# Product keys in a two-layer decoder: row one-hots kept two groups at a time, every key row in split form

## The chip, the core and the metric

The program runs on one core of a Trainium2 chip. The metric is the time of one execution on the device in microseconds (us). The engines are PE (matrix products; its weight loads are listed apart as PEld), DVE (vector), ACT (scalar activations and copies), POOL (GpSimd) and SP (which issues the transfers). They run in parallel, each its own instructions in order, and wait for one another through semaphores.

## What is computed

A decoder of two layers over x of 16 x 128 tokens, 256 wide: causal attention, attention to a context, a product-key layer, gated attention, aligned attention, and a mixture of 16 experts. The change touches the product-key layer alone. Cut to what matters, with 8 heads, nk = 64, k = 8:

```python
xn = batch_norm(inputs) * gamma + beta
q = (xn @ w_q.T).reshape(b, n, 2, h, kd).transpose(2, 0, 1, 3, 4)
sim = jnp.einsum('pbnhd,hkpd->pbnhk', q, keys)
s, i = jax.lax.top_k(sim, k)
...  # sums of the two halves' best, the best 8 of the 64 sums
scores, pk = jax.lax.top_k(all_scores, k)
idx = jnp.take_along_axis(all_idx, pk, axis=-1)
o = jnp.einsum('bnd,bnhkd->bnhk', inputs, key_in[idx])
o = gelu(o) * softmax(scores)
return jnp.einsum('bnhk,bnhkd->bnd', o, key_out[idx])
```

## The kernel before

Tokens are taken in 16 tiles of 128, two tiles (t = 0 and t = 1) to a pair, 8 pairs. The kernel doesn't gather: it computes the gelu of the products with all 4096 rows of key_in and multiplies them by a matrix of weights that is zero where a key isn't chosen. The stage (stage_product_keys, line 1982) has a preparation and then a loop over pairs, whose last turn is written out.

**Preparation.** key_in is turned by PE in 16 jobs (turn_in) of four 128 x 128 blocks. ACT rounds a job to fp32r (kiT high) and DVE subtracts (kiT low); of the rows 24 to 31 (SPLIT = 24) only a plain fp32 copy is kept, in kiT_rest: those four jobs (WHOLE) come ahead of the loop. The loop over pairs (line 2049, in_jobs) has two jobs in turns 0 to 3 and one in turns 4 to 7, and beside it normalises the tokens (ACT, fp_xn), turns them (PE) and collects statistics (DVE).

**A pair on PE.** Sixteen activation steps (activations, line 2361), each 2 rows of keys x 2 halves of the width, fill a bank that ACT empties with a gelu (L2447). A split row takes three fp32r products (split_product, line 583: high·high, high·low, low·high); in four steps, rows 24 to 31, it is one plain fp32 product (L2371). After step 0 the codes of the first tile are turned (turn_codes, L2354); after steps 3 to 6 come the similarities of the pair's second tile (SIMS_AT = 3). Then come four weight groups of the first tile (weight_group, L2391): a group is 16 of the 64 token columns of both halves, 64 small f16 products of row one-hots (row_hot, the stationary side) with column one-hots (col_hot). The next pair's similarities stand between them. Then the outputs of the first tile (L2404, f_out), with the second tile's four groups put between its 32 products at 23, 24, 26 and 28 (SECOND_AT), and last the outputs of the second tile (f_turn).

**A pair on DVE.** one_hot (line 2534) makes column one-hots (L2565 to L2570) and then all row one-hots of a tile in one instruction (L2573). choose (line 2458) finds the best keys from the similarities; weigh (line 2520) divides the exponentials that ACT made and releases the turning of codes. apply_weights (line 2576) multiplies each group's weights into gel, in two instructions (L2586); PE's groups 2 and 3 wait for the application of groups 0 and 1, whose banks they reuse, and the outputs for all four. The order is one_hot(0), choose(1), apply 0 of tile 0, weigh(1), apply 1 to 3, one_hot(1), apply of tile 1, residual, choose and weigh of the next pair.

**POOL** makes the low parts of the next pair's two inputs, xb_pair (L2284) and hT_pair (L2290), each as soon as ACT has rounded the high part.

## Time and profile before

| what | us |
|---|---|
| median of 3 runs | 2009.88 (2009.46 to 2011.67) |
| the profiled execution, own time | 2011.48 |
| its span | 2009.8 |
| PE busy in it | 1842.6 (92%) |
| DVE busy | 1327.1 (66%) |
| ACT busy | 649.5 (32%) |
| POOL busy | 175.8 (9%) |
| mean granted clock of PE | 0.964 |

The span runs from the first to the last instruction. A busy share is a mean over six stages with different limits. The product-key layer takes the time from 538 (preparation) over 582 (first pair) to 1141. In rows in order of time the first number is the start from the beginning of the span, the second the length in us; xN is the number of instructions merged in a row, and brackets give the idle time of the engine before it and what ended it. Granted clock 1.00 is 2.4 GHz, 0.5 is 1.2 GHz.

### The profile page before, as it was taken

The numbers are of one execution on the slowest core, as the hardware profiler recorded it, in microseconds if no ns is written. First come the engines' busy times: TensorE is split into PE (matmuls) and PEld (weight loads), VectorE is DVE, ScalarE is ACT, GpSimd is POOL, SyncE is SP. The second block draws the span as 40 slices with busy tenths as digits, with TensorE's granted clock in tenths as the row PEclk, the third lists the DMA queues.
The fourth block names the chain that finished last, engine by engine and source line by source line (L and its number), as shares of the span: only waits on it lengthen the run. The fifth ranks groups of instructions, "written<-read, shape, count | busy, mean of one in ns | idle before, by whom it ended". The sixth has DMA issues, their size and how long they took to land. (4 is left out here: it accounts for less than half of the span.)

```text
span 2009.8 us, 43767 instructions
## 1 busy us (share of the span) xinstructions
PE 1842.6 (92%) x16819; PEld 1541.4 (77%) x16819; DVE 1327.1 (66%) x3598; ACT 649.5 (32%) x1504; POOL 175.8 (9%) x125
## 2 busy tenths in 40 slices
PE   6999999699749999999999878878899999999998
PEld 5887787477638888888888645557788888888887
DVE  4555555377668988888988446646666666666664
ACT  3444434244342211221122035426333333323332
POOL 0000000011000000000000046531000000000000
PEclk9999999799879999999999879979899999999999
DMA  4000000222060000000000130001212010111101
GB/s 159 1 1 0 0 0 1 48 64 63 1 131 8 8 7 3 7 7 8 3 7 1 35 85 1 0 1 38 33 16 32 16 31 16 29 18 27 20 0 43
DMA packets 139319, 48.61 MB, mean 24 GB/s; under 512 B 108178, under 2 KB 138418, under 8 KB 139186
## 3 DMA queue, kind: packets, MB, share of 16 engines
q1 hardware_dynamic: 139186, 46.66, 10.4%
q8 instruction: 105, 1.72, 0.4%
q14 instruction: 28, 0.23, 0.0%
HBM read 42.43 MB, written 4.19 MB: 23 GB/s over the span
## 5 line engine op out<-in xcount | busy, mean ns | idle before, releaser
L2849 DVE TENSOR_TENSOR m_act_up<-m_silu,m_up 128x512 f32<-128x512 f32 x136 | 93.5, 687 | 168.0 <-PE m_up L587 125.0
L2768 ACT ACTIVATE m_silu<-m_gate 128x512 f32<-128x512 f32 x136 | 81.5, 599 | 379.6 <-PE m_gate L587 379.6
L2833 DVE SCALAR_TENSOR_TENSOR g_x<-m_y,m_combine,g_x 128x256 f32<-128x256 f32 x272 | 118.8, 479 | 52.8 <-PE m_y L587 51.3
L233 ACT ACTIVATE a_prob<-a_score,a_neg_max 128x128 f32<-128x128 f32 x256 | 90.7, 367 | 170.3 <-DVE a_neg_max L223 170.3
L2404 PE MATMUL f_out<-f_ko,f_gel 128*128 128x256 f32 x512 | 123.9, 394 | 2.4 <-issue 1.3
L2447 ACT ACTIVATE f_gel<-f_act 128x512 f32<-128x512 f32 x128 | 76.6, 598 | 131.7 <-PE f_act L587 90.9
L2404 PE MATMUL f_turn<-f_ko,f_gel 128*128 128x256 f32 x512 | 111.8, 379 | 0.0
L2404 PEld LDWEIGHTS f_out<-f_ko,f_gel 128*128 128x128 f32 x512 | 96.1, 194 | 17.1 <-issue 4.1
L587 PE MATMUL f_act<-f_hT_pair_high,f_kiT_high 128*128 128x256 f32 x384 | 108.2, 282 | 0.0
L2404 PEld LDWEIGHTS f_turn<-f_ko,f_gel 128*128 128x128 f32 x512 | 97.3, 190 | 13.2
L587 PE MATMUL f_act<-f_hT_pair_high,f_kiT_low 128*128 128x256 f32 x384 | 107.3, 279 | 0.0
L587 PE MATMUL f_act<-f_hT_pair_low,f_kiT_high 128*128 128x256 f32 x384 | 107.3, 279 | 0.0
L2839 DVE TENSOR_TENSOR m_hidden_low<-m_act_up,m_hidden_high 128x512 fp32r<-128x512 f32 x136 | 93.2, 685 | 1.5
L1281 POOL TENSOR_TENSOR a_inv<-a_ss,a_inv_power 128x64 f32<-128x64 f32 x8 | 84.6, 10571 | 71.7 <-DVE a_ss L1485 71.7
L2762 ACT CAST m_hidden_high<-m_act_up 128x512 fp32r<-128x512 f32 x136 | 83.4, 613 | 18.9 <-DVE m_act_up L2849 18.9
L587 PE MATMUL m_y<-g_wT_high,m_hidden_high 128*128 128x256 f32 x288 | 81.9, 284 | 2.9 <-DVE g_x L2833 1.9
L587 PE MATMUL m_y<-g_wT_high,m_hidden_low 128*128 128x256 f32 x288 | 81.8, 284 | 0.0
L587 PE MATMUL m_y<-g_wT_low,m_hidden_high 128*128 128x256 f32 x288 | 81.5, 283 | 0.0
L587 PE MATMUL a_ring<-a_xnT_high,a_w_high 128*128 128x256 f32 x256 | 77.1, 301 | 4.5 <-DVE a_w_low L544 4.4
L2437 ACT ACTIVATE g_shared<-g_shared 128x64 f32<-128x64 f32 x16 | 4.1, 256 | 235.8 <-DVE g_shared L2483 235.7
L587 PE MATMUL m_y<-m_wT_high,m_hidden_high 128*128 128x256 f32 x256 | 73.0, 285 | 1.9 <-DVE g_x L2833 1.9
L587 PEld LDWEIGHTS f_act<-f_hT_pair_high,f_kiT_high 128*128 128x128 f32 x384 | 72.0, 188 | 2.8 <-ACT f_gel L2447 1.4
(381 smaller groups left out, 5010.0 us busy)
## 6 DMA issues: line engine op xcount, KB each, us to landing
f_gel<-in_L_ffn_key_in SPq DMA_DIRECT2D x16, 256.0 KB, 4.9
f_ko<-in_L_ffn_key_out SPq DMA_DIRECT2D x2, 2048.0 KB, 18.5
g_shared<-in_ctx SPq DMA_DIRECT2D x8, 256.0 KB, 2.8
fp_wq_nat<-in_L_ffn_w_q SPq DMA_DIRECT2D x8, 256.0 KB, 3.1
h_kept<-fp_hT SPq DMA_DIRECT2D x8, 256.0 KB, 2.9
g_shared<-h_kept SPq DMA_DIRECT2D x8, 256.0 KB, 3.4
g_ctx_next<-in_ctx SPq DMA_DIRECT2D x8, 256.0 KB, 2.7
g_ctx_all<-in_ctx SPq DMA_DIRECT2D x1, 2048.0 KB, 10.3
```

What stands on the lines that cost most here:

```text
L233: last = act.activation(self.prob[:, u % 4, j, :], self.score_bank[u % 2][:, j // 2, (j % 2) * P:(j % 2 + 1) * P], ACT.Exp, bias=self.neg_ ...
L587: ins = pe.matmul(dst, left[a], right[b], start=first and n == 0, stop=last and n == 2)
L1281: pool.tensor_tensor(inv[par][:, :], ss[par][:, :], inv_power[:, :], ALU.pow).then_inc(inverse_ready, 1)
L2404: last = pe.matmul(out_of(t), gel[:, r, t * P:(t + 1) * P], ko[:, r, :], start=(r == 0), stop=(r == R - 1))
L2437: act.activation(weight[:, :, :], weight[:, :, :], ACT.Exp).then_inc(weight_exp, 1)
L2447: act.activation(gel[:, rows_of(u):rows_of(u) + 2, :].rearrange("p r t -> p (r t)"), act_bank[q][:, :], ACT.Gelu).then_inc(act_used[q].sem, 1)
L2762: act.copy(hidden[0][:, g % 2, m, :], act_up[:, m, :]).then_inc(high_ready[m].sem, 1)
L2768: act.activation(silu[:, m, :], gate_bank[m][:, :], ACT.Silu).then_inc(silu_ready[m].sem, 1)
L2833: last = dve.scalar_tensor_tensor(x[:, tile, :], y_bank[n][:, t * D:(t + 1) * D], weight, x[:, tile, :], ALU.mult, ALU.add)
L2839: dve.tensor_tensor(hidden[1][:, g % 2, m, :], act_up[:, m, :], hidden[0][:, g % 2, m, :], ALU.subtract).then_inc(low_ready[m].sem, 1)
L2849: dve.tensor_tensor(act_up[:, m, :], silu[:, m, :], up_bank[m][:, :], ALU.mult) \
```

## The change

All 32 rows of keys are kept in split form, kiT_rest is gone, and all sixteen activation steps are split products, in the order of the rows. The 16 turning jobs of the preparation all go through the loop, two in each turn. To make room, row_hot keeps two groups instead of four (8 KB less in each partition): DVE makes groups 0 and 1 in one instruction at the end of one_hot, and group m + 2 after it has applied group m, ahead of the weighing. PE waits for row one-hots (row_ready) at groups 2 and 3 too. POOL's low part of hT_pair also waits for the first row one-hots of the second tile of the pair before. The second tile's similarities come after steps 2 to 5.

```diff
-        self.kiT = [s.sb(f"kiT_{part}", [P, KD, self.SPLIT, P], F32R) for part in ("high", "low")]
-        self.kiT_rest = s.sb("kiT_rest", [P, KD, self.R - self.SPLIT, P])
+        self.kiT = [s.sb(f"kiT_{part}", [P, KD, self.R, P], F32R) for part in ("high", "low")]
...
-                if n < WHOLE:
-                    return n // 2, SPLIT + 4 * (n % 2)
-                return (n - WHOLE) // 6, 4 * ((n - WHOLE) % 6)
+                return n // 8, 4 * (n % 8)
...
-                return range(WHOLE + 2 * i, WHOLE + 2 * i + 2) if i < 4 else range(WHOLE + i + 4, WHOLE + i + 5)
+                return range(2 * i, 2 * i + 2)
...
-                for n in range(WHOLE):
-                    turn_in(n)
...
-                for n in range(WHOLE):
-                    k, r = in_rows(n)
-                    act.wait_ge(in_turned[n % 2], n // 2 + 1)
-                    act.copy(kiT_rest[:, k, r - SPLIT:r - SPLIT + 4, :].rearrange("p r c -> p (r c)"), in_bank[n % 2][:, :]) \
-                        .then_inc(in_done[n % 2], 1)
...
-        row_hot = s.sb("row_hot", [P, HALF, P], F16)
+        row_hot = s.sb("row_hot", [P, 2, GT, P], F16)
...
-        hot_ready = s.sem("hot_ready")
+        row_ready = s.counting("row_ready", GU - 1)
...
-        TURN_AT, SIMS_AT, SECOND_AT = 0, 3, (23, 24, 26, 28)
+        TURN_AT, SIMS_AT, SECOND_AT = 0, 2, (23, 24, 26, 28)
...
                     pool.wait_ge(h_high, i + 1)
+                    if not (isinstance(i, int) and i == 0):
+                        pool.wait_ge(row_ready.sem, row_ready.at(2 * i - 1, 1))
                     pool.tensor_tensor(hT_pair[1][:, :, :], h_pair[:, :, :], hT_pair[0][:, :, :],
                                        ALU.subtract).then_inc(h_low, 1)
...
-            return 2 * ((step + SPLIT // 2) % (R // 2))
+            return 2 * step
...
-                            if r < SPLIT:
-                                last = split_product(pe, dst, [part[:, k, r, :] for part in kiT],
-                                                     [part[:, k, :] for part in hT_pair], k == 0, k == KD - 1)
-                            else:
-                                last = pe.matmul(dst, kiT_rest[:, k, r - SPLIT, :], h_pair[:, k, :],
-                                                 start=(k == 0), stop=(k == KD - 1))
+                            last = split_product(pe, dst, [part[:, k, r, :] for part in kiT],
+                                                 [part[:, k, :] for part in hT_pair], k == 0, k == KD - 1)
...
-                    pe.wait_ge(hot_ready, n + 1)
+                    pe.wait_ge(row_ready.sem, row_ready.at(n, 1))
...
+                    if m >= 2:
+                        pe.wait_ge(row_ready.sem, row_ready.at(n, m))
...
-                                last = pe.matmul(weight_bank(m, q)[:, j * R:(j + 1) * R], row_hot[rows, GT * m + j, :],
+                                last = pe.matmul(weight_bank(m, q)[:, j * R:(j + 1) * R], row_hot[rows, m % 2, j, :],
...
+            def row_hots(at, groups):
+
+                slot = at % 2
+                dve.tensor_tensor(by_twos(row_hot[:, slot:slot + groups, :, :].rearrange("p m t c -> p (m t) c")),
+                                  per_token(code_twice[:, 0, GT * at:GT * (at + groups), :], P),
+                                  numbers(P, GT * groups), ALU.is_equal).then_inc(row_ready.sem, 1)
+
+            def next_row_hots(i, t, m):
+
+                n = 2 * i + t
+                for q in range(2):
+                    dve.wait_ge(g_ready[q].sem, g_ready[q].at(n, m + 1))
+                row_hots(m + 2, 1)
...
-                dve.tensor_tensor(by_twos(row_hot[:, :, :]), per_token(code_twice[:, 0, :, :], P), numbers(P),
-                                  ALU.is_equal).then_inc(hot_ready, 1)
+                row_hots(0, 2)
...
+                    if m + 2 < GU:
+                        next_row_hots(i, t, m)
                     after(m)
```

On DVE, in the loop over pairs, first tile, from the application of group 0 (f_g) to that of group 3 (f_act); f_weight_sum and g_shared are the weighing. Before:

```order
L2586 SCALAR_TENSOR_TENSOR f_gel<-f_g,f_gel 128x32x16 x2
L2526 TENSOR_REDUCE f_weight_sum<-g_shared 128x8
...
L2527 RECIPROCAL f_weight_sum<-f_weight_sum 128x8
...
L2529 SCALAR_TENSOR_TENSOR g_shared<-g_shared,f_weight_sum 128x64 x2
...
L2586 SCALAR_TENSOR_TENSOR f_gel<-f_act,f_gel 128x32x16 x2
...
L2586 SCALAR_TENSOR_TENSOR f_gel<-f_g,f_gel 128x32x16 x2
...
L2586 SCALAR_TENSOR_TENSOR f_gel<-f_act,f_gel 128x32x16 x2
```

and after the change:

```order
L2587 SCALAR_TENSOR_TENSOR f_gel<-f_g,f_gel 128x32x16 x2
L2535 TENSOR_TENSOR f_row_hot<-f_code_twice,f_iota_half 128x2048
L2514 TENSOR_REDUCE f_weight_sum<-g_shared 128x8
...
L2515 RECIPROCAL f_weight_sum<-f_weight_sum 128x8
...
L2517 SCALAR_TENSOR_TENSOR g_shared<-g_shared,f_weight_sum 128x64 x2
...
L2587 SCALAR_TENSOR_TENSOR f_gel<-f_act,f_gel 128x32x16 x2
L2535 TENSOR_TENSOR f_row_hot<-f_code_twice,f_iota_half 128x2048
...
L2587 SCALAR_TENSOR_TENSOR f_gel<-f_g,f_gel 128x32x16 x2
...
L2587 SCALAR_TENSOR_TENSOR f_gel<-f_act,f_gel 128x32x16 x2
```

Two row one-hot instructions of 128x2048 have moved in, one ahead of the weighing and one ahead of the application of group 2.

On PE, in the loop over pairs, the first matmul of the first tile's groups 0 to 3 (f_g and f_act in turn), the turning of codes and the first output, with what each waits for. Before:

```order
L2391 MATMUL f_g<-f_col_hot,f_row_hot 128x32 [waits f_col_ready,f_hot_ready]
...
L2391 MATMUL f_act<-f_col_hot,f_row_hot 128x32 [waits f_act_used1,f_act_used0]
...
L2391 MATMUL f_g<-f_col_hot,f_row_hot 128x32 [waits f_g_used1,f_g_used0]
...
L2391 MATMUL f_act<-f_col_hot,f_row_hot 128x32 [waits f_g_used1,f_g_used0]
...
L2354 MATMUL f_turn<-g_ident,g_shared 128x128 [waits f_codes_copied,f_codes_ready]
L2354 MATMUL f_turn<-g_ident,g_shared 128x128 x2
...
L2404 MATMUL f_out<-f_ko,f_gel 128x256 [waits f_out_used0,f_g_used1,f_g_used0]
```

and after the change:

```order
L2379 MATMUL f_g<-f_col_hot,f_row_hot 128x32 [waits f_col_ready,f_row_ready]
...
L2379 MATMUL f_act<-f_col_hot,f_row_hot 128x32 [waits f_act_used1,f_act_used0]
...
L2379 MATMUL f_g<-f_col_hot,f_row_hot 128x32 [waits f_row_ready]
...
L2379 MATMUL f_act<-f_col_hot,f_row_hot 128x32 [waits f_row_ready]
...
L2344 MATMUL f_turn<-g_ident,g_shared 128x128 [waits f_codes_copied,f_codes_ready]
L2344 MATMUL f_turn<-g_ident,g_shared 128x128 x2
...
L2392 MATMUL f_out<-f_ko,f_gel 128x256 [waits f_out_used0,f_g_used1,f_g_used0]
```

The groups stand where they stood; groups 2 and 3 now name row one-hots as what they wait for.

## Rows read from the trace of the kernel before

**Rows 1.** Windows: busy us (instructions) of PE, PEld, DVE, ACT, POOL; granted clock, DMA, GB/s.

```profile
665.50:732.90 67.40, 67.06 (x847) 58.94 (x847) 59.36 (x231) 14.68 (x24) 2.59 (x2) 1.00 0.02 6
...
1098.20:1105.20 7.00, 4.44 (x260) 3.88 (x259) 6.83 (x20) 2.14 (x3) 0.00 (x0) 0.94 0.02 5
1105.28:1118.30 13.02, 13.02 (x46) 10.74 (x46) 9.48 (x10) 0.00 (x0) 0.00 (x0) 0.77 0.00 1
```

**Rows 2.** Tile f_kiT_rest: count, duration ns min/median/max, first and last start.

```profile
L2371 PE MATMUL f_act<-g_shared,f_kiT_rest x256: 378/379/635, 582.3 to 1078.2; 128*128 128x256 f32 x128
```

**Rows 3.** ACT in order of time, the gelus; columns: start us, length us, instruction.

```profile
671.22 0.60 ACT L2447 ACTIVATE f_gel<-f_act 128x512 f32<-128x512 f32 x1 [1.13 <-PE f_act L2371]
672.94 0.60 ACT L2447 ACTIVATE f_gel<-f_act 128x512 f32<-128x512 f32 x1 [1.13 <-PE f_act L2371]
...
682.81 0.60 ACT L2447 ACTIVATE f_gel<-f_act 128x512 f32<-128x512 f32 x1 [0.81 <-PE f_act L587]
684.22 0.60 ACT L2447 ACTIVATE f_gel<-f_act 128x512 f32<-128x512 f32 x1 [0.81 <-PE f_act L587]
```

**Rows 4.** PE in order of time, first tile's weights and start of outputs.

```profile
692.85 0.96 PE L2391 MATMUL f_g<-f_col_hot,f_row_hot 64*128 64x32 f16 x64
...
696.43 0.97 PE L2391 MATMUL f_g<-f_col_hot,f_row_hot 64*128 64x32 f16 x64
...
698.44 1.01 PE L2391 MATMUL f_act<-f_col_hot,f_row_hot 64*128 64x32 f16 x64
...
700.86 10.17 PE L2404 MATMUL f_out<-f_ko,f_gel 128*128 128x256 f32 x46 [0.20 <-issue]
```

**Rows 5.** DVE in order of time, the same stretch.

```profile
693.85 1.29 DVE L2586 SCALAR_TENSOR_TENSOR f_gel<-f_g,f_gel 128x512 f32<-128x512 f32 x2 [0.19 <-PE f_g L2391]
...
695.65 1.44 DVE L2529 SCALAR_TENSOR_TENSOR g_shared<-g_shared,f_weight_sum 128x64 f32<-128x64 f32 x2
697.02 1.28 DVE L2586 SCALAR_TENSOR_TENSOR f_gel<-f_act,f_gel 128x512 f32<-128x512 f32 x2
698.22 1.27 DVE L2586 SCALAR_TENSOR_TENSOR f_gel<-f_g,f_gel 128x512 f32<-128x512 f32 x2
```

**Rows 6.** DVE, start of a choosing, last column one-hots, row one-hots.

```profile
680.00 0.06 DVE L2464 MEMSET f_spare<- 1x1 f32 x1 [2.15 <-PE f_sim L587]
...
705.25 1.23 DVE L2570 TENSOR_TENSOR f_col_hot<-f_col_hot,f_w_twice 128x2048 f16<-128x2048 f16 x1
706.39 4.42 DVE L2573 TENSOR_TENSOR f_row_hot<-f_code_twice,f_iota_half 128x8192 f16<-128x8192 f16 x1
```

**Rows 7.** POOL in order of time, the two subtractions.

```profile
687.94 1.29 POOL L2284 TENSOR_TENSOR f_xb_pair_low<-g_shared,f_xb_pair_high 128x512 fp32r<-128x512 f32 x1 [58.32 <-ACT f_xb_pair_high L2318]
695.71 1.30 POOL L2290 TENSOR_TENSOR f_hT_pair_low<-g_shared,f_hT_pair_high 128x512 fp32r<-128x512 f32 x1 [6.48 <-ACT f_hT_pair_high L2323]
```

**Rows 8.** PE, second tile's groups 0, 2 and 3 between output matmuls.

```profile
710.96 0.96 PE L2391 MATMUL f_g<-f_col_hot,f_row_hot 64*128 64x32 f16 x64
...
714.44 0.97 PE L2391 MATMUL f_g<-f_col_hot,f_row_hot 64*128 64x32 f16 x64
...
716.40 0.96 PE L2391 MATMUL f_act<-f_col_hot,f_row_hot 64*128 64x32 f16 x64
```

**Rows 9.** ACT in the preparation, first instruction of three turns.

```profile
558.10 1.12 ACT L2149 ACTIVATE fp_xn<-g_x,fp_token_shift,fp_token_rstd 128x256 f32<-128x256 f32 x2
...
560.52 1.14 ACT L2149 ACTIVATE fp_xn<-g_x,fp_token_shift,fp_token_rstd 128x256 f32<-128x256 f32 x2
...
562.45 1.15 ACT L2149 ACTIVATE fp_xn<-g_x,fp_token_shift,fp_token_rstd 128x256 f32<-128x256 f32 x2
```

**Rows 10.** DVE in the last pair, last instructions of the weighing.

```profile
1101.04 0.36 DVE L2529 SCALAR_TENSOR_TENSOR g_shared<-g_shared,f_weight_sum 128x64 f32<-128x64 f32 x2
```

**Rows 11.** PE in the last pair, group 0 and the outputs.

```profile
1098.24 0.96 PE L2391 MATMUL f_g<-f_col_hot,f_row_hot 64*128 64x32 f16 x64
...
1105.28 13.11 PE L2404 MATMUL f_out<-f_ko,f_gel 128*128 128x256 f32 x46 [1.09 <-DVE f_gel L2586]
```

## Prediction of the time after the change

> **What bounds the kernel now.** I read the page's busy shares first, then the stretch of stage windows, then one pair of tiles in order of time on PE and DVE. Over a middle pair, 67.4 us long, PE is busy 67.06 us at full granted clock, while DVE is busy 59.36 us [rows 1]. So PE sets the time of a pair, DVE has 8 us to spare in all, and what counts is where DVE's work stands. The eight pairs repeat one another closely, so one pair is worked out and multiplied. T below is the start of the first weight matmul of a pair's first tile (692.85 in the pair shown [rows 4]); W is the same of its second tile (710.96 [rows 8]).
>
> **The key rows.** Before, four of the sixteen activation steps of a pair are plain fp32: two records of PE for each matmul, 256 in all for 8 pairs of four steps with four matmuls each [rows 2]. ACT's gelus follow the steps, so their distance is PE's time for a step: 672.94 − 671.22 = 1.72 us for a plain one, 684.22 − 682.81 = 1.41 us for a split one [rows 3]. The change turns the four into split ones: 4 × (1.72 − 1.41) = 1.25 us off PE in each pair, 10.0 us in eight. Both ends are measured on the very engine, so I allow only 9.5 to 10.5. (In the first pair one of the four hides behind a wait for codes, but the clock is half there and the others save more.)
>
> The Trainium skill (FP8 and Floating Point Precision, section TensorE Precision Notes) says that true fp32 takes four passes through the array. A split product takes three. By that a split step would cost three quarters of 1.72, or 1.29 us, and four of them in eight pairs would save 13.8 us, not 10.0. The trace doesn't agree: the ratio is 0.82.
>
> **The preparation.** The four key blocks that were only copied (before the loop, while ACT waited for the token statistics anyway) now go through the loop as rounded ones, so turns four to seven of the loop do two jobs, not one. The loop runs at ACT's pace. Its turn with two jobs takes 560.52 − 558.10 = 2.42 us, with one 562.45 − 560.52 = 1.93 us [rows 9]. Four turns at 0.49 are +2.0 us, all on the path, since the stage's pairs begin only when it is over. Bounds: 1.5 (DVE's end unchanged) and 2.6 (one more remainder of DVE at the tail).
>
> **The row one-hots, first tile.** This is the part that decides. DVE made all four groups in one instruction of 4.42 us [rows 6], long before T. Now two groups are made early, and group 2 and group 3 each only after group 0 and group 1 have been applied, between the applications. The trace has no row one-hot of one group. The same kind of instruction on 128x2048 f16, the column one-hots, takes 1.23 us, and the next one starts 706.39 − 705.25 = 1.14 us after it [rows 6]; a quarter of 4.42 would be 1.11, with the start-up of each instruction left out. I take 1.22 busy and 1.14 between starts.
>
> DVE's order after the change: apply group 0, one-hots 2, the three instructions that weigh the second tile, apply 1, one-hots 3, apply 2, apply 3. Start to start, an application of two instructions costs 698.22 − 697.02 = 1.20 [rows 5]. The weighing costs 2.1 us before, because its last two instructions take 1.44 us [rows 5] while POOL's low part runs, 695.71 to 697.01 [rows 7]. In the last pair, where POOL has no low part to make, the same two take 0.36 us [rows 10]. The change makes POOL's low part wait for the second tile's one-hots, in the middle of the output matmuls, where DVE has nothing to do until W + 1. So the weighing costs 0.76.
>
> The Trainium skill (SBUF — State Buffer, section Who interferes with whom) says that a DVE instruction with both inputs in SBUF and a GpSimd one that reads SBUF lock each other out. The trace agrees: 0.36 against 1.44 us.
>
> The sum: application 0 starts at T + 1.00 as before [rows 4, 5]; one-hots 2 run from 2.21 to 3.43; PE may start group 2 at 3.54 and reaches it at 3.58 anyway, as before [rows 4], so nothing is lost there. Weighing from 3.35, application 1 at 4.11 (before 4.17), one-hots 3 from 5.32 to 6.54. PE starts group 3 at T + 6.64; before, 698.44 − 692.85 = 5.59 [rows 4]. Application 3 needs that group's last matmul, at 7.64: it runs 7.67 to 8.96, and the outputs, which wait for it, start at T + 9.04; before, 700.86 − 692.85 = 8.01 [rows 4]. **PE loses 1.03 us** in each of seven pairs, 7.2 us. In the last pair no similarities of a next pair fill PE's gaps and no POOL was in the way, so it started its outputs at 1105.28 − 1098.24 = 7.04 [rows 11]; the new chain of DVE gives the same 9.04, so that pair loses 2.0. Together +9.2 us. Bounds: with one-hots at 1.11 and no latency, 0.8 a pair; with 0.1 us for each added wait of DVE and PE, 1.3: 7.0 to 11.5.
>
> **The second tile.** From W: application 0 at 1.00, one-hots 2 ready at 3.43, PE on group 2 at 3.54 (before 714.44 − 710.96 = 3.48 [rows 8]); application 1 at 3.35, one-hots 3 from 4.56 to 5.78, PE on group 3 at 5.88 (before 716.40 − 710.96 = 5.44 [rows 8]). Everything behind it moves by 0.44 us: 8 × 0.44 = +3.5 us; bounds 0.3 and 0.6 each, 2.4 to 4.8. One-hots of two groups (2.3 us, between 1.23 and 4.42) end by T + 16.9 and PE asks for them at T + 19.1, so the later start of that chain costs nothing.
>
> **The second similarities.** Moved from step three to step two, with the saving, they end at some 2.7 us earlier on PE. DVE waited 2.15 us for them before choosing [rows 6], and from there to application 0 (693.85 [rows 5]) it went on without a wait but the last 0.2 us. The choosing takes some 13.7 us and now ends 1.6 us before application 0 (2.7 earlier on a T that is 1.25 earlier, and the 0.2). It costs PE nothing and buys slack alone. POOL's other subtraction (687.94, 1.29 us [rows 7]) now meets DVE's matching instructions, which read two tiles of SBUF; that can hold DVE by 0.7 us, and the slack covers it.
>
> **The sum:** −10.0 + 2.0 + 9.2 + 3.5 = **+4.7 us**. The profiled execution has a span of 2009.8 us and its own time 2011.48; the median of the runs is 2009.88, so I add to the median: **2014.6 us**. The bounds added in the same direction reach from about 2010.5 to 2019. A change within 0.2% (4.0 us) is about what a measurement of this kernel can't tell from none.
>
> **The rivals.**
> The granted clock falls. In the last pair PE is busy only 4.44 of 7.00 us around the weights, and then the clock falls: 46 records of outputs take 13.0 us at a mean of 0.77 instead of 10.1 in a middle pair [rows 1, 4, 11]: from 2.4 to 1.2 GHz for part of it. One fall costs 2.9 us. The change puts a gap of 1.4 us before group 3 and one of 0.35 before the outputs into every pair. Against: similarities and weights stand between the gaps, and PE stays busy some 7.3 of 9 us. If half of the pairs fall, +10 us: 2025; one fall is inside my own range. Chance 0.12.
> DVE is held by POOL while it chooses, and the slack isn't there: 0.7 × 7 = +5 us, 2019.5. It decides from 1.6 us of delay on. Chance 0.08.
> POOL's low part still meets the weighing (the change doesn't do what it says): 1.08 × 7 = +7.6, 2022. The order of POOL speaks against it. Chance 0.04.
> Split steps run by their number of passes, as three quarters of the plain ones: −13.8 in place of −10.0, 2010.8. The gelus' distances speak against it. Chance 0.04.
> DVE isn't late (the other side): PE never waits for one-hots 3. That takes their end by T + 5.4, where I have 6.54; if DVE's gaps hid 1.1 us there and 0.4 at the second tile, the two waits would vanish: 2009.9 − 10.0 + 2.0 + 1 = 2003. For it speaks only that DVE is less busy than PE; against it that from application 0 to the outputs DVE's rows show not one wait [rows 5]. Chance 0.08.
>
> **How the numbers follow.** The forecast has 0.61; about two thirds of it lie over 2013.9, one third between 2009 and 2013.9, by the bounds of the two waits. The rest, 0.03, is left for what I haven't thought of, near no change. Slower by over 0.2%: 0.40 + 0.12 + 0.08 + 0.04 = 0.64. Within 0.2%: 0.21 + 0.04 + 0.03 + a little of the last rival, 0.29. Faster: 0.07. The range leaves out the last rival and the clock's upper half: 2009.5 to 2023.
>
> **What would show it.** Right: gelus 1.41 apart in all sixteen steps; the weighing's two instructions at 0.36 us in every pair; PE idle about 1.4 us before group 3 of the first tile and 0.4 before that of the second, put down to DVE's row one-hots; outputs 9.0 us after T; the preparation 2.0 us longer; a pair of 67.6 us. Wrong: group 3 starting under T + 5.7; granted clock under 1.00 in the middle pairs; DVE choosing until application 0.

## The result, and the profile after the change

The changed kernel takes **2015.85 us** (median of 11 runs, 2012.65 to 2023.99); the kernel before, in as many runs beside it, 2009.46 (2007.41 to 2011.67). The ratio is 1.0036, 95% interval 1.0025 to 1.0046: slower by 0.36%, outside the 0.2% that count as no change. Run once more beside the experiments it took 2017.62 (ratio 1.0044, 1.0027 to 1.0061). The forecast was 2014.6, in 2009.5 to 2023, slower. Time and sign came out; two terms of the sum did not, and they are what the experiments are about.

The profiled execution of the changed kernel (span 2019.6) is one of its longer ones; that of the second measurement (span 2014.4) is called the second trace. First the windows of the changed kernel: from one second tile's first weight matmul to the next pair's, then the two pieces of the last pair, to be held against [rows 1]. Columns as there: busy us (instructions) of PE, PEld, DVE, ACT, POOL; granted clock, DMA, GB/s.

```profile
717.84:785.67 67.83, 66.16 (x863) 58.51 (x864) 59.09 (x234) 14.65 (x24) 2.55 (x2) 1.00 0.02 6
1106.73:1116.09 9.36, 4.79 (x261) 4.20 (x260) 8.19 (x16) 2.14 (x3) 0.00 (x0) 0.73 0.01 2
1116.09:1128.70 12.61, 12.61 (x46) 10.44 (x46) 7.35 (x10) 0.00 (x0) 0.00 (x0) 0.80 0.01 1
```

A pair grew from 67.4 to 67.8 us while PE's work in it fell from 67.06 to 66.16: PE now waits 1.7 us of it. Where, is seen on PE in order of time, first tile (answers to [rows 4]; start us, length us, instruction, idle time before it and what ended it):

```profile
698.73 0.96 PE L2379 MATMUL f_g<-f_col_hot,f_row_hot 64*128 64x32 f16 x64
...
702.32 0.97 PE L2379 MATMUL f_g<-f_col_hot,f_row_hot 64*128 64x32 f16 x64
...
705.30 0.96 PE L2379 MATMUL f_act<-f_col_hot,f_row_hot 64*128 64x32 f16 x64 [1.12 <-DVE f_row_hot L2535]
...
707.74 0.45 PE L2392 MATMUL f_out<-f_ko,f_gel 128*128 128x256 f32 x1 [0.25 <-issue]
```

With T = 698.73, group 2 starts at T + 3.59 (forecast 3.58), group 3 at T + 6.57 (6.64), the outputs at T + 9.01 (9.04; before 8.01). The 1.12 us ahead of group 3 are put down to the row one-hots. DVE in the same stretch (answers to [rows 5, 6]):

```profile
699.73 1.29 DVE L2587 SCALAR_TENSOR_TENSOR f_gel<-f_g,f_gel 128x512 f32<-128x512 f32 x2 [0.63 <-PE f_g L2379]
700.94 1.22 DVE L2535 TENSOR_TENSOR f_row_hot<-f_code_twice,f_iota_half 128x2048 f16<-128x2048 f16 x1
...
702.55 0.36 DVE L2517 SCALAR_TENSOR_TENSOR g_shared<-g_shared,f_weight_sum 128x64 f32<-128x64 f32 x2
702.83 1.28 DVE L2587 SCALAR_TENSOR_TENSOR f_gel<-f_act,f_gel 128x512 f32<-128x512 f32 x2
704.03 1.21 DVE L2535 TENSOR_TENSOR f_row_hot<-f_code_twice,f_iota_half 128x2048 f16<-128x2048 f16 x1
705.16 1.28 DVE L2587 SCALAR_TENSOR_TENSOR f_gel<-f_g,f_gel 128x512 f32<-128x512 f32 x2
...
713.23 2.28 DVE L2535 TENSOR_TENSOR f_row_hot<-f_code_twice,f_iota_half 128x4096 f16<-128x4096 f16 x1
```

The chain has no gap: one-hots of one group 1.22 us (1.13 start to start), of two 2.28, the weighing's last two instructions 0.36 instead of 1.44. POOL stands out of their way now (answer to [rows 7]), and the second tile loses 0.30 us ahead of its last group (answer to [rows 8]; W = 717.84, group 3 at W + 5.81, before 5.44):

```profile
715.59 1.27 POOL L2280 TENSOR_TENSOR f_hT_pair_low<-g_shared,f_hT_pair_high 128x512 fp32r<-128x512 f32 x1 [20.49 <-DVE f_row_hot L2535]
```

```profile
723.65 0.96 PE L2379 MATMUL f_act<-f_col_hot,f_row_hot 64*128 64x32 f16 x64 [0.30 <-DVE f_row_hot L2535]
```

**Where the time stands.** The product-key layer cut at starts that every trace has: first turning of keys, first similarity, W of the eight pairs, last output product (us):

| piece | before | changed | changed, second trace |
|---|---|---|---|
| preparation, to the first similarity | 38.16 | 43.90 | 40.68 |
| from there to W of the first pair | 66.38 | 66.10 | 65.99 |
| six periods from W to W | 405.34 | 407.96 | 409.08 |
| seventh period (into the last pair) | 69.45 | 70.72 | 70.16 |
| last W to the last output product | 21.77 | 22.32 | 22.32 |
| sum | 601.10 | 611.00 | 608.23 |

The layer begins at 538.98, 540.01 and 538.01 us, and the stages behind it take 869.7, 868.6 and 868.1 us, so they give 1.1 to 1.6 back. The preparation, forecast with +2.0, costs 2.5 in one trace and 5.7 in the other; it is the first open question. The second is the pairs. A period without a fall of the clock is 67.83; before, the six have a mean of 67.56, the shortest 67.40. The added waits of 1.00 and 0.37 us fit the forecast, so the key rows gave only 0.9 to 1.1 of the forecast 1.25 (1.37 less 0.43, held against the shortest period, or less 0.27, held against the mean).

### The profile page after: what moved, and what is told of

Same layout as the page of the kernel before. It is cut to its first block and busy times, and to the rows that moved or that the text cites. A ratio compares the mean times of both kernels' runs of the same rounds, so it can differ in the third digit from the quotient of the medians.

```text
span 2019.6 us, 44141 instructions
## 1 busy us (share of the span) xinstructions
PE 1841.8 (91%) x16947; PEld 1547.6 (77%) x16947; DVE 1327.6 (66%) x3634; ACT 648.6 (32%) x1504; POOL 176.3 (9%) x125
## 3 DMA queue, kind: packets, MB, share of 16 engines
q8 instruction: 105, 1.72, 0.3%
## 5 line engine op out<-in xcount | busy, mean ns | idle before, releaser
L587 PE MATMUL f_act<-f_hT_pair_high,f_kiT_high 128*128 128x256 f32 x512 | 147.0, 287 | 0.2
L587 PE MATMUL f_act<-f_hT_pair_low,f_kiT_high 128*128 128x256 f32 x512 | 144.0, 281 | 0.0
L587 PE MATMUL f_act<-f_hT_pair_high,f_kiT_low 128*128 128x256 f32 x512 | 144.0, 281 | 0.0
L587 PEld LDWEIGHTS f_act<-f_hT_pair_high,f_kiT_high 128*128 128x128 f32 x512 | 97.2, 190 | 4.7 <-ACT f_gel L2435 1.6
L587 PEld LDWEIGHTS f_act<-f_hT_pair_low,f_kiT_high 128*128 128x128 f32 x512 | 97.1, 190 | 1.6
L587 PEld LDWEIGHTS f_act<-f_hT_pair_high,f_kiT_low 128*128 128x128 f32 x512 | 97.4, 190 | 0.0
```

What stands on the lines that cost most here:

```text
L587: ins = pe.matmul(dst, left[a], right[b], start=first and n == 0, stop=last and n == 2)
```

## Experiments

Each runs beside the kernel before on the same chip; every diff is against the changed kernel, unless it says otherwise. The periods are from W to W; "layer" is the sum of the table above (changed 611.0 and 608.2, before 601.1).

### The changed kernel again

> The changed kernel once more, as the reference for the others on the same chip. Its first trace has the preparation (from its first turning of keys to the first similarity) at 43.91 us, before 38.16: 5.75 longer, where the prediction had 2.0. If that excess belongs to the kernel, this execution shows 43 to 44 again, with the granted clock at half through the first 20 us of the preparation; if it was chance of one execution, 40 to 41. In the pairs: third group 3.6 and fourth 6.6 us behind the first tile's first weight matmul, outputs at 9.0, a pair of 67.8 us. Total 2014 to 2018.

Measured: 2017.62 us; preparation 40.68. So the excess has more than one size in one and the same kernel. The turnings of key_in and the fused products (of the keys with w_q, 128x64 each on PE) tell them apart. Before:

```profile
540.84 3.76 PE L2086 MATMUL fp_in_bank<-g_ident,f_gel 128*128 128x128 f32 x16
544.39 3.80 PE L2093 MATMUL fp_key_bank<-fp_keysT,fp_wq_nat 128*128 128x64 f32 x32
```

Changed, first trace, PE, then ACT behind it:

```profile
542.62 7.09 PE L2088 MATMUL fp_key_bank<-fp_keysT,fp_wq_nat 128*128 128x64 f32 x32 [0.68 <-ACT fp_keysT L2128]
549.50 1.91 PE L2081 MATMUL fp_in_bank<-g_ident,f_gel 128*128 128x128 f32 x8
551.21 3.52 PE L2088 MATMUL fp_key_bank<-fp_keysT,fp_wq_nat 128*128 128x64 f32 x16
```

```profile
554.76 0.59 ACT L2124 CAST f_fused_high<-fp_key_bank 128x512 fp32r<-128x512 f32 x1 [2.48 <-PE fp_key_bank L2088]
...
559.45 0.59 ACT L2124 CAST f_fused_high<-fp_key_bank 128x512 fp32r<-128x512 f32 x1 [1.55 <-PE fp_key_bank L2088]
```

Second trace:

```profile
540.62 7.09 PE L2088 MATMUL fp_key_bank<-fp_keysT,fp_wq_nat 128*128 128x64 f32 x32 [0.68 <-ACT fp_keysT L2128]
547.50 1.88 PE L2081 MATMUL fp_in_bank<-g_ident,f_gel 128*128 128x128 f32 x8
549.21 1.91 PE L2088 MATMUL fp_key_bank<-fp_keysT,fp_wq_nat 128*128 128x64 f32 x16
```

The same 16 products take 1.91 or 3.52 us. The first 18 us of the preparation as windows (columns as above; the granted clock is the third number from the end), before, changed and second trace:

```profile
538.98:556.98 18.00, 16.61 (x129) 15.65 (x130) 12.65 (x45) 11.53 (x22) 2.98 (x2) 0.84 0.01 2
```

```profile
540.01:558.01 18.00, 17.32 (x89) 17.14 (x90) 10.78 (x42) 7.03 (x13) 2.99 (x2) 0.50 0.01 1
```

```profile
538.01:556.01 18.00, 16.79 (x112) 16.37 (x112) 12.49 (x45) 8.64 (x17) 2.98 (x2) 0.69 0.01 1
```

Before, the clock was at 1.2 GHz until 5.7 us into the preparation and at 2.4 for the rest of these 18 us; now it stays at 1.2 for 11.2 or for 18.0 us. A rise at 11.2 costs some 0.4 us: ACT starts its first turn 10.22 us into the preparation instead of 10.04, since the second fused product comes later, and its second turn 3.40 us behind the first instead of 3.14. One at 18.0 makes ACT wait longer for the third and fourth fused product and costs another 3.2 us. Six profiled executions have this preparation unchanged: these two and four of the experiments below (one-hots in three groups, POOL early, similarities, turning). The rise came at 11.2 us in two of them (40.7 us), at 12.5 in one (41.3), at 17.9 or 18.0 in three (43.9). The changed kernel's runs spread over 11 us and those before over 4; these 3.2 us can be only a part of that, and the rest isn't explained.

### Two jobs ahead of the fused products

```diff
+            AHEAD = 2
...
-                return range(2 * i, 2 * i + 2)
+                return range(AHEAD + 2 * i, AHEAD + 2 * i + 2) if i < 6 else range(AHEAD + i + 6, AHEAD + i + 7)
...
+                for n in range(AHEAD):
+                    turn_in(n)
                 pe.wait_ge(keys_copied, 2)
```

with the matching copies of ACT ahead of its fused products and DVE's low parts ahead of its wait for POOL.

> The changed kernel with two of the 16 turning jobs ahead of the fused products (in split form, as all of them), so that six turns of the loop have two jobs and two have one; nothing else differs. Clock theory: with the transposes gone from ahead of the fused products PE's activity there is too thin, the clock rises only 13 us later than before, and the fused products run at half of it; eight transposes ahead bring a part or all of that back, so the preparation shrinks by 2.5 to 4.7 us (to 39.2 to 41.4), with the clock up before 550. Jobs theory: the excess is the price of jobs in the loop alone, so that two turns fewer with two jobs give 2 x 0.49 = 1.0 us (to 42.9) and the clock rises as late as in the changed kernel.

Measured: 2019.32 us; preparation 40.62, clock up at 12.5 us. Neither theory held as put: eight transposes did not bring the clock back, and two turns fewer with two jobs (−1.0) were paid for by the two jobs ahead at 1.2 GHz, which put off the second fused product, for which ACT's first turn waits (it starts 11.07 us into the preparation, not 10.22; the second turn is 3.60 us behind it, not 3.40).

### Dummy transposes

```diff
+                for n in range(4):
+                    for j in range(4):
+                        pe.transpose(in_bank[0][:, j * P:(j + 1) * P], gel[:, j, 0:P], ident[:, :])
                 pe.wait_ge(keys_copied, 2)
```

> The changed kernel with 16 dummy transposes on PE between the turning of the keys and the fused products, where before four turning jobs stood; their results are overwritten by the first real job. So far the granted clock rose 5.7 us after the start of the preparation in the kernel before, 11.2 us after it in two executions of the changed form and 18.0 us after it in two others, where the preparation took 40.7 and 43.9 us (before 38.2). Activity theory: what PE does ahead of and in the fused products decides when the clock rises; with the transposes back it rises near 5.7 again in every execution, the fused products run at the full clock but start 2.8 us later, and the preparation takes 40.2 to 40.8 us, never 43.9. Chance theory: the moment has nothing to do with these instructions; then it rises at 11 or 18 again, and with 3.8 us more of half-clock work ahead the preparation takes 43 to 47 us.

Measured: 2015.49 us; the clock rises 4.3 us in, preparation 40.24. As activity theory said. So the 16 transposes matter, whatever they turn. And with the clock up early and all 16 jobs in the loop the preparation is 2.08 us longer than before (38.16), which is the forecast's +2.0 by itself.

### Four real jobs ahead

```diff
+            AHEAD = 4
+
+            def bank(n):
+                return pair_bank[n % 2] if 2 <= n < AHEAD else in_bank[n % 2]
...
-                return range(2 * i, 2 * i + 2)
+                return range(AHEAD + 2 * i, AHEAD + 2 * i + 2) if i < 4 else range(AHEAD + i + 4, AHEAD + i + 5)
...
+                for n in range(AHEAD):
+                    turn_in(n)
                 pe.wait_ge(keys_copied, 2)
```

with ACT's and DVE's part of the four ahead as well.

> The changed kernel with four turning jobs in split form ahead of the fused products, as many as stood there before (the third and fourth into the two banks of the token pairs, which are free then), DVE making their low parts in the 3 us in which it waits for POOL's power; the loop has two jobs in four turns and one in four, as before. Activity theory of the clock: 16 transposes ahead of the fused products (so in three executions of three) let it rise 4 to 6 us after the start of the preparation. With the number of jobs in the loop as before too, the preparation takes 38.2 to 38.8 us (changed kernel 40.7 or 43.9), of which 1.9 are the four jobs fewer. Rival: what counts is the 2 us of extra work ahead, as with two jobs ahead (40.6): then 40 or more, and a rise at 11 us or later. Total 2012 to 2014.

Measured: **2013.21 us** (ratio 1.0011, 1.0002 to 1.0020); preparation 38.15, as before the change (38.16), layer 605.8. PE and DVE:

```profile
540.53 1.97 PE L2087 MATMUL fp_in_bank<-g_ident,f_gel 128*128 128x128 f32 x8
542.30 1.91 PE L2087 MATMUL fp_pair_bank<-g_ident,f_gel 128*128 128x128 f32 x8
544.00 3.84 PE L2094 MATMUL fp_key_bank<-fp_keysT,fp_wq_nat 128*128 128x64 f32 x32
```

```profile
545.31 1.28 DVE L2183 TENSOR_TENSOR f_kiT_low<-fp_in_bank,f_kiT_high 128x512 fp32r<-128x512 f32 x2
546.51 1.28 DVE L2183 TENSOR_TENSOR f_kiT_low<-fp_pair_bank,f_kiT_high 128x512 fp32r<-128x512 f32 x2
```

The clock rises 5.7 us in, the fused products run at full clock for the most part again (3.84 us for 32 of them), and the four low parts lie where DVE had nothing to do. Its runs still spread over 8 us (2009.82 to 2018.13). Over all profiled executions: with 16 transposes ahead of the fused products (before, and five experiments) the clock rose 4.3 to 5.7 us into the preparation, six of six; with none or eight (two of the changed kernel, and six experiments) at 11.2 to 18.8, eight of eight. That the transposes decide is shown; what it is about them isn't.

### Only the row part, on the kernel before

The kernel before with row_hot of two groups, row_ready and POOL's wait, nothing else of the change.

> The kernel before with only the row part of the change: two groups of row one-hots kept, the waits of PE for them, and POOL's low part held back; the four plain fp32 steps, the preparation and the place of the similarities stay as they were. Additive theory: the outputs of the first tile 1.0 us later (9.0 behind the first weight matmul), the second tile's fourth group 0.37 later, so a pair of 68.8 us instead of 67.4, over 2 us more in the last pair, preparation 38.2: +12 to +14 us. The other parts are then worth the difference to the changed kernel: by the gelus' distances the key rows would be worth 1.25 us in a pair, by the starts of the turning and of the weights in the two traces only 0.9 to 1.0. If a pair comes out at 69.1 the former holds, at 68.75 to 68.85 the latter. Rival: where the steps are plain, DVE's lateness is partly covered, a pair of 68.2 or less.

Measured: 2019.91 us (layer 615.25). Outputs at T + 9.0, group 3 at W + 5.81, preparation 38.16, an undisturbed period 68.80:

```profile
920.94:989.74 68.80, 67.24 (x848) 58.97 (x848) 58.09 (x234) 14.65 (x24) 2.56 (x2) 1.00 0.02 6
```

Additive, as expected: +1.4 for the waits, and the rest of the change is worth 68.80 − 67.83 = 0.97 us in a pair, not 1.25. That names the failed term, not yet its reason.

### The turning of codes one step later

```diff
-        TURN_AT, SIMS_AT, SECOND_AT = 0, 2, (23, 24, 26, 28)
+        TURN_AT, SIMS_AT, SECOND_AT = 1, 2, (23, 24, 26, 28)
```

> The changed kernel with the first tile's codes turned behind step one instead of step zero. In its trace step zero and the turning behind it start 1.68 us apart, in the kernel before (plain step) 1.72, so splitting this step gave 0.04 us and not 0.31. Waiting theory: the turning reuses the bank that DVE's last residual still reads, DVE comes to it only at the end of its choosing, and PE waits for it; one step later nobody waits, so 0.16 us come back in each of seven pairs (67.67 instead of 67.83), step zero taking 1.52 us; DVE, which is then 1.4 us later with the first one-hots, has 1.9 us of idle time ahead of its next choosing. Border theory: the time is the price of going from rounded products to plain ones and back, wherever that stands: a pair of 67.8 as before.

Measured: periods without a fall 67.55 to 67.57, so **−0.27** in a pair (expected −0.16), which decides for waiting. (The total, of this single run, 2018.94, has a preparation of 43.9 and three falls of the clock in it.) PE at the start of a pair, step 0 and the turning; first the kernel before:

```profile
732.94 1.89 PE L2371 MATMUL f_act<-g_shared,f_kiT_rest 128*128 128x256 f32 x8
734.66 0.49 PE L2354 MATMUL f_turn<-g_ident,g_shared 128*128 128x128 f32 x3
```

the changed kernel (second trace), where the twelve products of the step are issued 0.12 us apart and the last one starts at 804.10:

```profile
802.70 0.38 PE L587 MATMUL f_act<-f_hT_pair_high,f_kiT_high 128*128 128x256 f32 x1
...
804.10 0.28 PE L587 MATMUL f_act<-f_hT_pair_high,f_kiT_low 128*128 128x256 f32 x1
804.38 0.52 PE L2344 MATMUL f_turn<-g_ident,g_shared 128*128 128x128 f32 x3
```

and DVE there, before and in the second trace:

```profile
734.05 0.42 DVE L2593 TENSOR_TENSOR g_x<-f_turn,g_x 128x256 f32 x1
```

```profile
803.81 0.42 DVE L2596 TENSOR_TENSOR g_x<-f_turn,g_x 128x256 f32 x1
805.03 0.42 DVE L2556 CAST f_code_twice<-f_turn 64x256 f16<-64x256 f32 x1 [0.81 <-PE f_turn L2344]
```

PE may turn only when DVE has read the bank with its residual add (in turn_codes, a wait for out_used of the second tile), and DVE gets to that only at the end of its choosing; the add ends at 804.23. Before, it was over at 734.47 and the step at 734.66: the two were level, the wait did not show. The split step ends earlier and meets it: 1.68 us to the turning instead of 1.72. That DVE sets the time is seen across the pairs of the changed kernel's two traces: in the eleven of fourteen where the add came last, step 0 starts 22.2 to 22.4 us after W and lasts 1.60 to 1.85 us up to the turning, which each time starts 0.15 us behind the add, and the next T is 48.7 us after W. With the turning behind step one nobody waits (the turning is 1.2 to 1.5 us behind the add), step 0 takes 1.52 in most pairs, the next T is 48.5 us after W in most, and the four split steps are worth 67.83 − 67.56 + 0.97 = 1.24 us, the forecast's 1.25. The kernel before with the same shift wasn't run.

### Three groups of row one-hots

```diff
-        row_hot = s.sb("row_hot", [P, 2, GT, P], F16)
+        row_hot = s.sb("row_hot", [P, 3, GT, P], F16)
...
-                    if m >= 2:
-                        pe.wait_ge(row_ready.sem, row_ready.at(n, m))
+                    if m >= 3:
+                        pe.wait_ge(row_ready.sem, row_ready.at(n, m - 3 + 2))
...
-                slot = at % 2
+                slot = at % 3
...
-                row_hots(m + 2, 1)
+                row_hots(m + 3, 1)
...
-                row_hots(0, 2)
+                row_hots(0, 3)
...
-                    if m + 2 < GU:
+                    if m + 3 < GU:
```

The room comes from three small tiles of the choosing (match, rank, index) that move into the shared region.

> The changed kernel with three groups of row one-hots kept instead of two (matching scratch and two small index tiles moved into the shared region to make room), so that only the fourth group is made between applications, after the first. Theory of the row one-hots (two waits of PE for DVE in each pair, 1.0 and 0.4 us): the second instruction of 1.2 us leaves the chain, PE's fourth group starts at the end of application 1 again, 5.5 us behind the first one, the outputs at 7.9 (now 9.0) and the second tile's fourth group 5.4 behind its first (now 5.8): 1.1 + 0.4 us in each pair, more than 2 in the last: -12 to -14 us together. Rival: PE's clock or its queue sets the distance of the groups, the waits only change their name: within 2 us of the changed kernel.

Measured: 2006.09 us (ratio 0.9975, 0.9961 to 0.9988), layer 597.5, though its preparation was the long one, 43.89. Group 3 and the outputs of the first tile (T = 763.28):

```profile
768.89 0.97 PE L2381 MATMUL f_act<-f_col_hot,f_row_hot 64*128 64x32 f16 x64 [0.18 <-DVE f_gel L2589]
...
771.28 10.17 PE L2394 MATMUL f_out<-f_ko,f_gel 128*128 128x256 f32 x46 [0.20 <-issue]
```

T + 5.61 and T + 8.00, the second tile's group 3 at W + 5.44: both waits for row one-hots are gone, and a period is 66.3 to 66.5. −1.3 to −1.5 in each pair is what the forecast had put on the two waits (1.03 + 0.44).

### POOL's low part as early as before

```diff
-                    if not (isinstance(i, int) and i == 0):
-                        pool.wait_ge(row_ready.sem, row_ready.at(2 * i - 1, 1))
```

> The changed kernel without POOL's new wait, so that the low part of the next pair's input is made as soon as ACT has rounded it, as before the change. Lock theory: the weighing's last two instructions take 1.44 us again instead of 0.36, and since they stand ahead of application 1, the outputs start 1.0 to 1.1 us later in seven pairs: +7 to +7.6 us. Rival: with the similarities one step earlier POOL's operation falls elsewhere (while DVE chooses or makes one-hots), the weighing stays at 0.36 and the time within 1.5 us.

Measured: 2022.82 us; periods 68.42 (67.83), outputs at T + 9.60. POOL, then DVE:

```profile
769.61 1.71 POOL L2278 TENSOR_TENSOR f_hT_pair_low<-g_shared,f_hT_pair_high 128x512 fp32r<-128x512 f32 x1 [6.48 <-ACT f_hT_pair_high L2311]
```

```profile
770.58 0.95 DVE L2515 SCALAR_TENSOR_TENSOR g_shared<-g_shared,f_weight_sum 128x64 f32<-128x64 f32 x2
```

The two still meet, but the one-hots now stand ahead of the weighing, so DVE comes to it with POOL's operation more than half done: 0.59 us a pair instead of 1.08. The direction was right, the size expected too large.

### The similarities where they were

```diff
-        TURN_AT, SIMS_AT, SECOND_AT = 0, 2, (23, 24, 26, 28)
+        TURN_AT, SIMS_AT, SECOND_AT = 0, 3, (23, 24, 26, 28)
```

> The changed kernel with the second tile's similarities behind steps three to six, as before the change. In the changed kernel DVE is done with choosing 0.63 us before application 0 can start. Slack theory: a step is 1.41 us, so choosing ends 0.78 us too late, and in seven pairs application 0, the fourth group and the outputs all come 0.7 to 0.8 us later: outputs 9.75 behind the first weight matmul, +5 to +5.5 us. Rival: the earlier step bought nothing that matters (DVE's choosing has hidden idle time in it): outputs at 9.0, within 1 us.

Measured: 2018.52 us; undisturbed periods 67.8 to 67.9, outputs at T + 9.01: the rival. Moving them bought nothing. DVE ahead of application 0 (T = 695.74), and one cast of its choosing:

```profile
692.41 0.23 DVE L2482 CAST f_best_key_half<-f_best_key 128x128 f16<-128x128 uint32 x1
...
696.74 1.29 DVE L2587 SCALAR_TENSOR_TENSOR f_gel<-f_g,f_gel 128x512 f32<-128x512 f32 x2 [0.19 <-PE f_g L2379]
```

The same cast in the changed kernel (second trace), and POOL at that moment:

```profile
756.53 1.21 DVE L2482 CAST f_best_key_half<-f_best_key 128x128 f16<-128x128 uint32 x1
```

```profile
756.36 1.29 POOL L2272 TENSOR_TENSOR f_xb_pair_low<-g_shared,f_xb_pair_high 128x512 fp32r<-128x512 f32 x1 [44.83 <-ACT f_xb_pair_high L2308]
```

A step earlier is 1.41 us, but the choosing then meets POOL's subtraction and one cast takes 1.0 us longer: the idle time ahead of application 0 is 0.63 us with the move and 0.19 without, and neither holds PE up.

### Versions that put the findings together

Three groups, two jobs ahead, and ACT's second fused rounding behind its first normalisation:

> Candidate: three groups of row one-hots, two turning jobs ahead of the fused products (two turns of the loop fewer with two jobs), and ACT rounding the second fused product behind the first pair's normalisation instead of ahead of it, so that the 2 us which the two jobs cost at half clock aren't waited for. The pairs as with three groups alone: 66.3 us each, no wait for row one-hots. Preparation 39.8 to 40.2 us if its clock rises by 12.5 us after its start (three groups alone: 43.9 with a rise at 18.0). Total 2000 to 2003; if the two jobs ahead give nothing again, 2003 to 2006.

Measured: 2006.55 us (ratio 0.9986, 0.9977 to 0.9996). The pairs came as expected (66.45), the clock rose 18.8 us in, preparation 43.67. Eight transposes ahead don't do.

Three groups and four real jobs ahead:

> Three groups of row one-hots and this preparation together. If the two causes are apart and add: pairs of 66.3 us, no fall of the clock between the first pair and the last one's outputs, preparation 38.2 to 38.8 us, so the layer from the start of its preparation to the last output takes 583.7 - 43.9 + 38.5 = 578.3 us (before 587.3), and the total comes out at 1999 to 2002, 0.4 to 0.5% under the kernel before. If the preparation's clock rises late all the same, 2003 to 2006.

Measured: 2002.80 us (ratio 0.9956, 0.9943 to 0.9970), preparation 38.17, layer 593.0: 8.1 us under before, expected 9.0. The two causes are apart and add.

The same with the turning behind step one:

> The fastest kernel so far (three groups of row one-hots, four turning jobs ahead) with the same shift of the turning by one step. Waiting theory: up to 0.16 us in each of seven pairs (66.3 instead of 66.45): a stage of 578.2 instead of 579.2 us, total 1 us less, 2001 to 2003. Border theory: the same within 0.3 us of the stage.

Measured: **1999.46 us** (1998.68 to 2000.98; ratio 0.9957, 0.9939 to 0.9974), layer 589.9, preparation 38.17, periods 66.2 to 66.5. The preparation, and a stretch as long as a pair (from 0.5 us ahead of a W), as windows:

```profile
537.63:555.63 18.00, 16.30 (x129) 15.40 (x130) 15.03 (x49) 11.42 (x22) 2.99 (x2) 0.88 0.01 2
704.38:770.56 66.18, 65.80 (x863) 58.47 (x862) 58.91 (x232) 14.67 (x24) 2.46 (x3) 1.00 0.02 6
```

It keeps what the change was good for, all key rows split, and beats both kernels. It was measured beside the kernel before alone; against the changed kernel go their two ratios (0.9957, and 1.0036 or 1.0044). Whether it also beats the version without the shift can't be told from the ratios; its trace is 3.1 us shorter in the layer, 1.4 of them ahead of the first W.

## Why the prediction came out as it did

**Row one-hots and POOL (+9.2 and +3.5): right, by their mechanism.** First tile +1.03 forecast, 9.01 − 8.01 = 1.00 measured; second 0.44 forecast, 0.37 measured; the weighing at 0.36; one-hots 1.22 and 2.28. Three groups take both waits away and give 1.4 us a pair back, which shows it. In the last pair T to the outputs grew by 9.36 − 7.04 = 2.3 (forecast 2.0), and the outputs behind took 0.4 less.

**Key rows (−10.0): the saving is real, 0.27 us of it in a pair was lost.** The term was the difference of two gelus' distances times four. It holds for three steps: from the turning to T 24.72 us instead of 25.62. The fourth, step 0, ends at a wait that was level with it before. Taken as measured the term is 0.97 × 8 = −7.8: 2.2 us short, and outside the bounds of 9.5 to 10.5. The forecast looked for who is late next at the one-hots and did not look at the turning of codes.

**Preparation (+2.0): the mis-sized term.** Its loop came out as forecast: in the second trace turns with two jobs 2.42 us apart to the end, 40.68 − 38.16 = 2.5, inside the bounds of 1.5 to 2.6, and 40.24 − 38.16 = 2.1 where the clock rises early all the same (dummy transposes). But the forecast called the four jobs ahead free, in both directions. They were work that stood ahead of the fused products, and without them the clock came up 5.5 or 12.3 us later: 0.4 us in the second trace, another 3.2 us in the first, which is 5.7 for the forecast's 2.0 and outside its bounds. Put back, 38.15.

**The second similarities: harmless, and useless.** Forecast: 1.6 us of slack, 0.7 of it taken by POOL. Measured: 0.63 us of slack, POOL's share 1.0. Without the move PE is no worse.

**The rivals.** The granted clock did fall within the pairs, each time to 1.2 GHz for 3.4 us that begin 6.9 to 9.0 us after T, right behind the added gap. The prediction had named a granted clock under 1.00 in the middle pairs as a sign of being wrong, so this sign came: in one pair of seven in the first trace, in two in the second. Such a fall costs 0.9 to 1.2 us (a period of 68.70 or 68.99 instead of 67.83), not the 2.9 that the forecast took from the last pair; nine executions with two groups kept show 18 of them in 63 pairs, five with three or four groups kept show none in 35. At that price two of them, 2.1 us, stay inside the range; the rival (half of the pairs, +10 us) did not come. PE in one such place of the second trace, where three similarity products stand 0.39 to 0.43 us apart instead of 0.23 to 0.34:

```profile
971.31 0.96 PE L2379 MATMUL f_act<-f_col_hot,f_row_hot 64*128 64x32 f16 x64 [1.13 <-DVE f_row_hot L2535]
972.21 0.60 PE L587 MATMUL f_sim<-f_fused_high,f_xb_pair_high 128*128 128x512 f32 x1
972.60 0.63 PE L587 MATMUL f_sim<-f_fused_low,f_xb_pair_high 128*128 128x512 f32 x1
973.03 0.63 PE L587 MATMUL f_sim<-f_fused_high,f_xb_pair_low 128*128 128x512 f32 x1
```

DVE held by POOL while choosing: happened, 1.0 us, covered by the slack. Split steps by their passes (three quarters of a plain one): no, gelus 1.41 us apart after the change, too (first trace):

```profile
743.82 0.60 ACT L2435 ACTIVATE f_gel<-f_act 128x512 f32<-128x512 f32 x1 [1.16 <-PE f_act L587]
745.23 0.60 ACT L2435 ACTIVATE f_gel<-f_act 128x512 f32<-128x512 f32 x1 [0.81 <-PE f_act L587]
```

DVE not late: no, PE waited 1.12 and 0.30 us for its one-hots.

**Why the total was near all the same.** The layer of the second trace is +7.1 us where the sum had +4.7. By pieces, held against the forecast's terms for each:

- The preparation costs 0.5 more (2.5 for 2.0).
- The six periods cost 2.4 more (3.7 for 1.3). The two falls are 2.1 of it. Each period is 0.18 longer beside that, 1.1 in all: the key rows gave 0.28 less, the waits took 0.1 less. Against it, three of the six periods before were themselves 0.2 to 0.3 longer than 67.43, which takes 0.8 off.
- The first pair up to its W gives 0.2 more (0.4 for 0.2).
- The last pair, from the W ahead of it, costs 0.4 less (1.3 for 1.6).

That layer began 1.0 us earlier than the one before, and the stages behind give 1.6 back; neither was forecast, so the trace ends 4.6 us over the one before. That this is the sum's +4.7 is luck. The median is +6.4; the profiled execution before was 2.0 us over its median, so the two distances aren't the same thing. A late rise of the clock, 3.2 us, comes on top in a part of the executions; how often in those that make the median isn't known. What shortened the later stages wasn't tried; their clock changes level at other places in every trace.

## What to carry to other kernels

Work that is moved away from a stretch where the clock is low is not free because nobody waits for it: look at what the granted clock does there, and what ran ahead of its rise. Time saved on one engine in front of a wait that is level with it can be lost again (0.27 of 1.24 us here): follow each saving to the next instruction that waits for another engine and compare the two times in the trace. And where a buffer is cut, try first how few slots the chain needs: three of four one-hot groups left no wait for one-hots here, two cost 1.4 us a pair.

## What the runs showed of the hardware

- A granted clock that rises 4.3 to 5.7 us or 11.2 to 18.8 us into the same stage, by whether 16 transposes of 128x128 run ahead of 32 products of 128x64. PE was not less busy at the low clock (17.3 of 18 us against 16.6).
- In one and the same kernel the rise came at 11.2 us in one execution and at 18.0 in another; this alone moves its time by 3.2 us.
- A DVE cast of 128x128 from uint32 to f16, with one input, took 1.21 us instead of 0.23 while POOL subtracted two tiles in SBUF. The Trainium skill (SBUF — State Buffer, section Who interferes with whom) names casts among the instructions that can take the ports shared with GpSimd. By that rule, the trace agrees.
- Both can lose by the meeting: POOL's subtraction took 1.71 us instead of 1.27 where DVE's one-hots and then its weighing ran beside it (POOL early), the weighing 0.95 instead of 0.36. Where POOL met the weighing alone [rows 5, 7] it took 1.30, the weighing 1.44.
- In stretches with a wait of 1.1 us or more ahead of the fourth group of small f16 products, the granted clock fell for 3.4 us in 18 of 63 pairs; without that wait in none of 35.
